# Cross-attention and gated low-rank layer on one core: two turns moved within TensorE's order of a step

## The chip, the cores and the metric

One core of one Trainium2 chip runs the kernel. The metric is the device time of one execution in microseconds (us). The kernel before takes 184.85 us, the median of 3 runs (184.71 to 184.86).

## The reference

1024 tokens (16 batches of 64) of 512 numbers go through two layers, in float32:

```python
x = x + xattn(layernorm(x), ctx, ctx, positions, Wq, Wk, Wv, Wo)
x = x + ffn(layernorm(x), A_w, B_w, Wq_w, keys)
# xattn: 32 heads of 16, 8 heads of k and v; q and k are rotated by position; softmax over 64 keys
# ffn:
q = x @ Wq_w.T; scores = q @ keys.T              # 64 experts
gate = softmax of the 16 largest scores, spread back over the 64
z = x @ A_w.T                                    # 64 experts x rank 8
out = (z * gate) @ B_w.T * 2
```

## The kernel before, in words

The tokens are cut into 8 tiles of 128. A program per engine is written out by hand, and semaphores join them: each `wait_ge` stands in its engine's own order, so a waiting instruction holds up everything behind it on that engine.

Every large product is made in three passes, with both operands split into a rounded high part and a low remainder: high by high, high by low, low by high. `high_part` (L1037 to L1040) issues the first two passes, 8 matmuls of 128x512 for four chunks, and `low_part` (L1042 to L1045) the third, 4 matmuls. ScalarE makes the high part from PSUM, VectorE or GpSimd the low one.

A "turn" is a transpose of 128x128 on TensorE against the identity, with its result in PSUM: `turn_xh` (normalised x, 4 of them, into `ps_t1` in the steps spoken of here), `turn_k` (rotated k, 1, `ps_t0`), `turn_m` (the row maxima of the scores in `m_split`, 2, `ps_t0`), `turn_q`, `turn_x2`, `turn_zg` (gated z, 4, `ps_t1`).

The work is pipelined over the tiles. `first()` and `second()` fill the pipeline, `step(i)` runs for i = 1 to 5, and `last()` empties it. In `step(i)` TensorE works on up to four tiles: the attention of tile i, the scores of n = i+1, the projections of p = i+2, the x turn of i+3, and the gated layer of f = i-2. In step 1 there is no f, so the down product, the turn of z and the up product are left out; in step 5 there is no tile p+1, so the last turn, `turn_xh`, is left out. TensorE's order in `step(i)` before the change is, for i of 2 to 5:

1. `turned_scores(i)` (L1112 to L1126): waits for `mT_ok`, then makes the scores a second time, turned, in tiles of 32 rows, with the negative maxima `mT` added in.
2. `project_down(f, 0)`, `project_q(p, [0, 1])`, `project_down(f, 1)`, `turn_x2(i-1)`.
3. `values(i)`, `turn_q(n)`, `project_kv(p)`, `project_q(p, [2])`.
4. `scores(n, 0)`, `scores(n, 1)`, `turn_zg(f)`.
5. `project_q(p, [3])`, then `turn_k(p)`, then `project_out(i)`.
6. `up_high(f)`, which waits for `q_rot` (VectorE has rotated q of p); `turn_m(n)`, behind a wait for `kT_lo_ok`; `up_low(f)`; `turn_xh(p+1)`.

The next step begins with `turned_scores(i+1)`. What it waits for is made by ScalarE: `m_out(n)` (L486 to L491) copies the turned maxima from PSUM to `mT`. In ScalarE's step stand, in this order: four exponentials with `expert_scores` between the third and the fourth, the z copies, `x2_high`, `q_high`, `values_out`, `o_high`, `k_high(p)` (L472 to L476), `z_high`, `normalise`, `c_high`, `value_blocks`, `m_out(n)`, `x2_centre(i)`, `x_high(p+1)`.

VectorE's step: `x_low`, the statistics of x, `route(f)` (the 16 largest), `x2_low` (L822), `attend(i)` with `q_low(n)` in it, `rotate_k(p)` (L720 to L727), four maxima of the scores (L761), `k_low(p)` (L733), `rotate_q(p)` (L742, L744), `m_parts(n)` (L771, L773), `z_low(f)` (L884), `residual(i)`, `statistics2(i)`, `result(f)`. GpSimd's: `deviation1`, `gated`, `deviation2`, `o_low`, `k_blocks` of the high and of the low part, `rotated_q`, `c_low`. The loads and stores are on SyncE's queue and none of them is in the part of the program that is changed.

Of the kernel before, what the change touches and what calls it, by code (L numbers as in the profile page):

```python
# [51 lines left out]
def build(nc, x, cT, pos, wq, wkv, wo, aT, router, bT, out):  # L52
    ctx = ExitStack()
    with ctx:
# [114 lines left out]
        def kT_bank(t):  # L169
            return (ps_t1 if t < RAW else ps_t0)[:, 0:P]  # L170
# [4 lines left out]
        def up_of(t):  # L175
            return (ps_w0 if t < T - 2 else ps_w1)[:]
# [852 lines left out]
        def _(pe):  # L1029
            def product(dst, hi, lo, w_hi, w_lo, cols, chunks=range(DK)):  # L1030
                for k in chunks:
                    pe.matmul(dst, hi(k), w_hi[:, k, cols], start=(k == 0), stop=False)  # L1032
                    pe.matmul(dst, hi(k), w_lo[:, k, cols], start=False, stop=False)  # L1033
                    mm = pe.matmul(dst, lo(k), w_hi[:, k, cols], start=False, stop=(k == DK - 1))  # L1034
                return mm

            def high_part(dst, hi, w_hi, w_lo, cols, chunks=range(DK)):  # L1037
                for k in chunks:
                    pe.matmul(dst, hi(k), w_hi[:, k, cols], start=(k == 0), stop=False)  # L1039
                    pe.matmul(dst, hi(k), w_lo[:, k, cols], start=False, stop=False)  # L1040

            def low_part(dst, lo, w_hi, cols):  # L1042
                for k in range(DK):
                    mm = pe.matmul(dst, lo(k), w_hi[:, k, cols], start=False, stop=(k == DK - 1))  # L1044
                return mm  # L1045

            def chunk(t):
                return lambda k: t[:, k, :]

            def turn(dst, src, n):  # L1050
                for k in range(n):
                    mm = pe.transpose(dst[:, P * k:P * (k + 1)], src[:, P * k:P * (k + 1)], ident[:])  # L1052
                return mm
# [5 lines left out]
            def turn_xh(t):  # L1059
                pe.wait_ge(xh_ok, t + 1)  # L1060
                turn(xhT_bank(t), xh, DK).then_inc(xhT_ps, 1)

            def project_kv(t):
                if t == RAW:
                    pe.wait_ge(wkv_l, DK)
                pe.wait_ge(c_hi_ok, t - RAW + 1)
                high_part(ps_w1[:, 0:2 * KV], chunk(cT_hi), wkv_hi, wkv_lo, slice(0, 2 * KV))
                pe.wait_ge(c_lo_ok, t - RAW + 1)
                low_part(ps_w1[:, 0:2 * KV], chunk(cT_lo), wkv_hi, slice(0, 2 * KV)).then_inc(kv_ps, 1)

            def turn_k(t):
                pe.wait_ge(k_rot, 3 * t + 3)
                pe.transpose(kT_bank(t), k_r[:], ident[:]).then_inc(kT_ps, 1)

            def project_q(t, chunks):
                if t == RAW:
                    pe.wait_ge(wq_l, DK)
                pe.wait_ge(x_hi_ok, t - RAW + 1)
                pe.wait_ge(x_lo_ok, t - RAW + 1)
                return product(ps_w0[:], chunk(xT_hi), chunk(xT_lo), wq_hi, wq_lo, slice(0, D), chunks)  # L1080

            def turn_q(t):
                pe.wait_ge(q_r_ok, t + 1)
                turn(ps_t0, q_r, REP).then_inc(qT_ps, 1)
# [20 lines left out]
            def turn_m(t):  # L1105
                pe.wait_ge(m_lo_ok, t + 1)
                for rp in range(2):
                    mm = pe.transpose(mT_bank(t)[:, P * rp:P * (rp + 1)],  # L1108
                                      m_split[:, rp].bitcast(F32).rearrange("p c j n -> p (c j n)"), ident[:])
                mm.then_inc(m_ps, 1)  # L1110

            def turned_scores(t):  # L1112
                pe.wait_ge(mT_ok, t + 1)
                for b in range(2):
                    for n, (k, q) in enumerate(((k_bd_hi, qT_hi), (k_bd_lo, qT_hi), (k_bd_hi, qT_lo))):
                        for c in range(PAIRS):
                            rows = slice(QUAD * c, QUAD * (c + 1))
                            pe.matmul(ps_s[:, c, 2 * P * b:2 * P * (b + 1)],  # L1118
                                      k[rows, t % 2, b, 2 * (c % 2):2 * (c % 2) + 2, :].rearrange("p h k -> p (h k)"),
                                      q[rows, t % 2, b].rearrange("p r q -> p (r q)"),  # L1120
                                      start=(n == 0), stop=False)
                    for c in range(PAIRS):
                        rows = slice(QUAD * c, QUAD * (c + 1))
                        mm = pe.matmul(ps_s[:, c, 2 * P * b:2 * P * (b + 1)], sel[rows, b, :],  # L1124
                                       mT[rows].rearrange("p r q -> p (r q)"), start=False, stop=True)
                mm.then_inc(sT_ps, 1)  # L1126

            def values(t):
                pe.wait_ge(exp_ok, 4 * t + 4)
                pe.wait_ge(v_bd_ok, 4 * t + 4)  # L1130
                for b in range(2):
                    for c in range(PAIRS):
                        for h in range(2):
                            rows = slice(ROWS * h, ROWS * (h + 1))
                            mm = pe.matmul(ps_o[QUAD * c:QUAD * (c + 1), h, 2 * P * b:2 * P * (b + 1)],  # L1135
                                           v_bd[rows, t % 2, b, c, :], eT[rows, c, b, :], start=True, stop=True)
                mm.then_inc(o_ps, 1)
# [12 lines left out]
            def project_out(t):  # L1150
                out_high(t)
                out_low(t)

            def turn_x2(t):
                pe.wait_ge(x2_c_ok, t + 1)
                turn(x2T_bank(t), x2_c, DK).then_inc(x2T_ps, 1)
# [12 lines left out]
            def project_down(t, half):  # L1169
                down_high(t, half)  # L1170
                down_low(t, half)

            def turn_zg(t):
                pe.wait_ge(zg_ok, t + 1 if t < T - 1 else T + 1)
                turn(ps_t1, zg, DK).then_inc(zT_ps, 1)

            def up_high(t, chunks=range(DK)):
                if t == 0:
                    pe.wait_ge(b_l, DK)
                pe.wait_ge(zT_hi_ok, t + 1)  # L1180
                high_part(up_of(t), chunk(zT_hi), b_hi, b_lo, slice(0, D), chunks)

            def up_low(t):
                pe.wait_ge(zT_lo_ok, t + 1)
                low_part(up_of(t), chunk(zT_lo), b_hi, slice(0, D)).then_inc(up_ps, 1)
# [72 lines left out]
            def step(i):  # L1258
                f, g, n, p = i - 2, i - 1, i + 1, i + 2
                turned_scores(i)  # L1260
                if f >= 0:
                    pe.wait_ge(x2_ok, i)
                    project_down(f, 0)
                    if f >= 1:
                        pe.wait_ge(res_ok, f)
                    else:
                        pe.wait_ge(q_rot, 2 * p)
                    project_q(p, [0, 1])
                    pe.wait_ge(z_ok, 2 * f + 1)
                    project_down(f, 1)  # L1270
                    turn_x2(g)
                else:
                    pe.wait_ge(q_rot, 2 * p)
                    project_q(p, [0, 1, 2])
                    turn_x2(g)
                values(i)
                turn_q(n)
                if f >= 0:
                    pe.wait_ge(z_ok, 2 * f + 2)
                else:  # L1280
                    pe.wait_ge(x2_ok, i)
                project_kv(p)
                if f >= 0:
                    project_q(p, [2])
                scores(n, 0)
                scores(n, 1)
                pe.wait_ge(x2T_lo_ok, i)
                if f >= 0:
                    turn_zg(f)
                project_q(p, [3]).then_inc(q_ps, 1)  # L1290
                turn_k(p)
                pe.wait_ge(v_st_ok, p + 1)
                project_out(i)
                if f >= 0:
                    pe.wait_ge(q_rot, 2 * p + 2)
                    up_high(f)
                pe.wait_ge(kT_lo_ok, p + 1)
                turn_m(n)
                if f >= 0:
                    up_low(f)  # L1300
                if p + 1 < T:
                    turn_xh(p + 1)

# [64 lines left out]
            for i in range(1, T - 2):  # L1368
                step(i)
# [37 lines left out]
```

## Time and profile before

| what | value |
|---|---|
| median of 3 runs | 184.85 us (184.71 to 184.86) |
| profiled execution, its own time | 184.47 us |
| its span, first to last instruction | 182.5 us |
| granted TensorE clock | 1.00 of full speed throughout |
| TensorE busy (matmuls) | 169.6 us, 93% |
| VectorE busy | 133.0 us, 73% |
| ScalarE busy | 90.0 us, 49% |
| GpSimd busy | 85.6 us, 47% |

A row of the timeline gives the start in us from the span's start, the duration, the engine, the source line, the operation, output and inputs, the shape and how many like it are merged. In square brackets stands how long the engine was idle before the row and what ended that. PE is TensorE's matmuls, PEld its weight loads (a separate track that overlaps the matmuls), ACT ScalarE, DVE VectorE, POOL GpSimd. Matmuls are pipelined: the distance from one start to the next is what a matmul costs, and its duration is longer. A merged row of several matmuls begins with the first and ends with the last one's end. The name `late` is a buffer with four uses (a weight, the second x, z and the gated z).

### The profile page before, as it was taken

To read this page: it belongs to the slowest core of one execution; us is meant where nothing else is said; L and a number is where in the kernel's file an instruction comes from. 1 tells how busy PE (TensorE), PEld (TensorE's weight loads), DVE (VectorE), ACT (ScalarE), POOL (GpSimd) and SP (SyncE) were. 2 spreads that over 40 slices of the span, in tenths; PEclk is the share of its full clock that TensorE was granted. 3 is DMA by queue.
4 is the path that set the end of the run, shared out by engine and by line. 5 is a ranking of instruction groups with operands and counts; after the bars stand their busy time and mean duration, and the time that the engine had idled before them with its cause. 6 is when DMAs were issued, how large, how long until landed. Compare 5 with 4: busy or idle time off the path is not lost.

```text
span 182.5 us, 4057 instructions
## 1 busy us (share of the span) xinstructions
PE 169.6 (93%) x1440; PEld 130.9 (72%) x1440; DVE 133.0 (73%) x391; ACT 90.0 (49%) x206; POOL 85.6 (47%) x109
## 2 busy tenths in 40 slices
PE   7999999988969999999999999999997999599874
PEld 2656575666749887888788878978695767499653
DVE  2667858978994999569954997569938969465461
ACT  3579899636456534742665274644272360432210
POOL 5599989599488349131840275035503020603000
PEclk9999999999999999999999999999999999999999
DMA  5999802001101010101010000100010001000111
GB/s 180 300 400 392 348 4 59 2 12 49 61 3 54 4 57 0 63 0 57 5 57 0 4 0 0 63 0 0 4 57 0 4 0 57 4 4 0 57 57 58
DMA packets 5331, 11.30 MB, mean 62 GB/s; under 512 B 688, under 2 KB 944, under 8 KB 5056
## 3 DMA queue, kind: packets, MB, share of 16 engines
q1 hardware_dynamic: 5024, 10.79, 16.7%
q10 hardware_dynamic: 288, 0.27, 0.4%
q8 instruction: 11, 0.18, 0.4%
q14 instruction: 8, 0.07, 0.1%
HBM read 8.95 MB, written 2.10 MB: 61 GB/s over the span
## 4 chain that ended last, share of the span: by engine, by line
PE 57%; POOL 18%; DVE 10%; issue 10%; DMA 2%; ACT 1%; DVEq 0%; POOLq 0%
PE ps_w L1039 10%; PE ps_w L1044 10%; PE ps_w L1040 9%; PE ps_t L1052 6%; PE ps_s L1099 5%; POOL am_lo L268 3%; PE ps_s L1135 3%; PE ps_s L1118 3%; POOL wo_lo L268 3%; POOL wq_lo L268 2%; PE ps_w L1032 2%; PE ps_w L1033 2%; PE ps_w L1034 2%; POOL k_bd_hi L301 2%; POOL k_bd_lo L301 2%
## 5 line engine op out<-in xcount | busy, mean ns | idle before, releaser
L325 POOL TENSOR_TENSOR late<-late,gate 128x512 f32<-128x512 f32 x7 | 7.6, 1081 | 45.0 <-DVE gate L854 39.3
L310 POOL TENSOR_TENSOR oT_lo<-o_n,oT_hi 128x512 fp32r<-128x512 f32 x8 | 10.3, 1285 | 29.2 <-ACT oT_hi L505 29.2
L761 DVE TENSOR_REDUCE ps_s<-ps_s 128x8 f32<-128x512 f32 x32 | 20.8, 693 | 1.0 <-PE ps_s L1099 0.7
L497 ACT ACTIVATE eT<-ps_s 128x512 f32<-128x512 f32 x32 | 17.0, 598 | 4.1 <-PE ps_s L1124 4.0
L1039 PE MATMUL ps_w<-b_hi,zT_hi 128*128 128x512 f32 (+1 forms) x32 | 12.8, 405 | 1.6 <-ACT zT_hi L545 1.6
L1039 PE MATMUL ps_w<-am_hi,x2T_hi 128*128 128x288 f32 x48 | 13.9, 311 | 0.0
L1040 PE MATMUL ps_w<-am_lo,x2T_hi 128*128 128x288 f32 x48 | 13.1, 296 | 0.0
L505 ACT ACTIVATE oT_hi<-o_n 128x512 fp32r<-128x512 f32 x8 | 5.1, 634 | 14.4 <-DVE o_n L794 14.4
L1040 PE MATMUL ps_w<-b_lo,zT_hi 128*128 128x512 f32 (+1 forms) x32 | 12.1, 381 | 0.0
L1039 PE MATMUL ps_w<-wo_hi,oT_hi 128*128 128x512 f32 x28 | 11.7, 419 | 0.4 <-ACT oT_hi L505 0.4
L1200 PE MATMUL ps_w<-wq_sb,xT_raw 128*128 128x512 f32 x24 | 11.8, 606 | 0.0
L1099 PE MATMUL ps_s<-k_bd_hi,qT_hi 64*128 64x256 f32 x64 | 10.2, 311 | 1.3 <-issue 1.3
L545 ACT ACTIVATE zT_hi<-ps_t 128x512 fp32r<-128x512 f32 x8 | 4.8, 595 | 13.2 <-PE ps_t L1052 13.2
L1040 PE MATMUL ps_w<-wo_lo,oT_hi 128*128 128x512 f32 x28 | 11.1, 395 | 0.0
L779 DVE STREAM_TRANSPOSE o_s<-ps_s 128x1024 f32<-128x1024 f32 x8 | 9.9, 1241 | 0.6 <-PE ps_s L1135 0.6
L1099 PEld LDWEIGHTS ps_s<-k_bd_hi,qT_hi 64*128 64x128 f32 x64 | 6.2, 186 | 5.8 <-issue 5.8
L490 ACT ACTIVATE mT<-ps_t 128x256 fp32r<-128x256 f32 x8 | 3.1, 384 | 14.3 <-PE ps_t L1108 14.3
L1039 PEld LDWEIGHTS ps_w<-am_hi,x2T_hi 128*128 128x128 f32 x48 | 9.0, 187 | 1.2
L291 POOL TENSOR_TENSOR q_r<-q_a,q_b 128x512 f32<-128x512 f32 x7 | 9.0, 1292 | 1.5 <-DVE q_b L744 1.5
L1039 PEld LDWEIGHTS ps_w<-b_hi,zT_hi 128*128 128x128 f32 x32 | 6.0, 188 | 4.8 <-DVE q_b L744 1.8
L301 POOL TENSOR_TENSOR k_bd_lo<-kT_lo,half_mask 128x512 fp32r<-128x512 f32 x8 | 8.8, 1096 | 1.3 <-DVE kT_lo L733 1.3
L1135 PE MATMUL ps_s<-eT,v_bd 64*32 64x256 f32 x256 | 8.8, 382 | 0.6 <-ACT eT L497 0.6
(203 smaller groups left out, 526.4 us busy)
## 6 DMA issues: line engine op xcount, KB each, us to landing
x_sb<-x SPq DMA_DIRECT2D x8, 256.0 KB, 7.2
cT_in<-cT SPq DMA_DIRECT2D x7, 256.0 KB, 2.7
out<-res SPq DMA_DIRECT2D x7, 256.0 KB, 2.0
wq_sb<-wq SPq DMA_DIRECT2D x4, 256.0 KB, 6.4
late<-wo SPq DMA_DIRECT2D x1, 1024.0 KB, 8.3
am_sb<-aT SPq DMA_DIRECT2D x1, 1024.0 KB, 8.5
b_sb<-bT SPq DMA_DIRECT2D x1, 1024.0 KB, 7.1
wkv_sb<-wkv SPq DMA_DIRECT2D x1, 512.0 KB, 4.9
```

Of the source, the lines that this page charges most:

```text
L268: pool.tensor_tensor(lo[:, k, :], raw[:, k, :], hi[:, k, :].bitcast(F32), ALU.subtract).then_inc(low, 1)
L301: pool.tensor_tensor(bd[:, t % 2], kT[:].bitcast(F32).rearrange("p (b q) -> p b q", b=2).unsqueeze(2) .broadcast_to([P, 2, HALF_H, BATCH]) ...
L310: pool.tensor_tensor(oT_lo[:], o_n[:].rearrange("p (b r q) -> p r b q", b=2, r=REP), oT_hi[:].bitcast(F32), ALU.subtract).then_inc(oT_lo_o ...
L497: act.activation(eT[:, c].rearrange("p b n -> p (b n)"), ps_s[:, c, :], ACT.Exp)\
L761: dve.tensor_reduce(neg_top[:, b, HALF_H * half:HALF_H * (half + 1), :], ps_s[:, 2 * (1 - b) + half, :].rearrange("p (r h k) -> p h r k", ...
L1039: pe.matmul(dst, hi(k), w_hi[:, k, cols], start=(k == 0), stop=False)
L1040: pe.matmul(dst, hi(k), w_lo[:, k, cols], start=False, stop=False)
L1044: mm = pe.matmul(dst, lo(k), w_hi[:, k, cols], start=False, stop=(k == DK - 1))
L1052: mm = pe.transpose(dst[:, P * k:P * (k + 1)], src[:, P * k:P * (k + 1)], ident[:])
L1099: mm = pe.matmul(ps_s[:, 2 * (1 - b) + half, 2 * P * rp:2 * P * (rp + 1)], q[rows, t % 2, b, 2 * rp:2 * rp + 2, :].rearrange("p r q -> p ( ...
L1135: mm = pe.matmul(ps_o[QUAD * c:QUAD * (c + 1), h, 2 * P * b:2 * P * (b + 1)], v_bd[rows, t % 2, b, c, :], eT[rows, c, b, :], start=True, s ...
L1200: return pe.matmul(ps_w0[:], xT_raw[:, k, :], wq_sb[:, k, :], start=(k == 0), stop=(k == DK - 1))
```

## The change

`turn_k(p)` goes from behind `project_q(p, [3])` to ahead of it, directly behind `turn_zg(f)`. `up_low(f)` goes from behind `turn_m(n)` to directly behind `up_high(f)`, so that `turn_m(n)` stands directly ahead of `turn_xh(p+1)`. Nothing is added or removed, and no other engine's program changes.

```diff
@@ -1287,17 +1287,16 @@
                 pe.wait_ge(x2T_lo_ok, i)
                 if f >= 0:
                     turn_zg(f)
+                turn_k(p)
                 project_q(p, [3]).then_inc(q_ps, 1)
-                turn_k(p)
                 pe.wait_ge(v_st_ok, p + 1)
                 project_out(i)
                 if f >= 0:
                     pe.wait_ge(q_rot, 2 * p + 2)
                     up_high(f)
+                    up_low(f)
                 pe.wait_ge(kT_lo_ok, p + 1)
                 turn_m(n)
-                if f >= 0:
-                    up_low(f)
                 if p + 1 < T:
                     turn_xh(p + 1)
```

## Rows read from the trace of the kernel before

**Rows 1.** The page: the busy time of TensorE, and the clock it was granted

```profile
PE 169.6 (93%) x1440; PEld 130.9 (72%) x1440; DVE 133.0 (73%) x391; ACT 90.0 (49%) x206; POOL 85.6 (47%) x109
...
PEclk9999999999999999999999999999999999999999
```

**Rows 2.** The list of waits: engine, tile, line, released by: us in total, times, longest

```profile
PEld ps_w L1039 <- DVE q_b L744: 1.8, 4, 0.4
...
ACT late L533 <- PE ps_w L1044: 5.2, 4, 1.6
...
DVE x2T_lo L822 <- ACT x2T_hi L518: 5.8, 5, 1.5
```

**Rows 3.** Timeline of TensorE's matmuls, end of step 4 and start of step 5

```profile
111.21 0.39 PE L1040 MATMUL ps_w<-b_lo,zT_hi 128*128 128x512 f32 x1
111.44 0.38 PE L1108 MATMUL ps_t<-ident,m_split 128*128 128x128 f32 x2
111.58 1.18 PE L1044 MATMUL ps_w<-b_hi,zT_lo 128*128 128x512 f32 x4
112.59 0.60 PE L1052 MATMUL ps_t<-ident,xh 128*128 128x128 f32 x4
113.12 0.39 PE L1118 MATMUL ps_s<-qT_hi,k_bd_hi 32*128 32x256 f32 x4
```

**Rows 4.** Timeline of ScalarE, the same stretch

```profile
111.86 0.38 ACT L490 ACTIVATE mT<-ps_t 128x256 fp32r<-128x256 f32 x1 [2.21 <-PE ps_t L1108]
...
113.23 0.60 ACT L447 ACTIVATE xT_hi<-ps_t 128x512 fp32r<-128x512 f32 x1 [0.23 <-PE ps_t L1052]
114.38 1.57 ACT L497 ACTIVATE eT<-ps_s 128x512 f32<-128x512 f32 x3 [0.56 <-PE ps_s L1124]
```

**Rows 5.** Timeline, end of step 1 (no up product there), TensorE, its loads and ScalarE

```profile
53.22 0.41 PE L1108 MATMUL ps_t<-ident,m_split 128*128 128x128 f32 x2 [1.38 <-DVE m_split L773]
...
53.46 0.60 PE L1052 MATMUL ps_t<-ident,xh 128*128 128x128 f32 x4
...
53.66 0.38 ACT L490 ACTIVATE mT<-ps_t 128x256 fp32r<-128x256 f32 x1 [2.14 <-PE ps_t L1108]
...
54.10 0.19 PEld L1118 LDWEIGHTS ps_s<-qT_hi,k_bd_hi 32*128 32x128 f32 x4 [0.28 <-ACT mT L490]
...
54.70 0.58 ACT L447 ACTIVATE xT_hi<-ps_t 128x512 fp32r<-128x512 f32 x1
```

**Rows 6.** Timeline, end of step 5 and start of the last part

```profile
131.11 0.38 PE L1108 MATMUL ps_t<-ident,m_split 128*128 128x128 f32 x2
...
131.53 0.38 ACT L490 ACTIVATE mT<-ps_t 128x256 fp32r<-128x256 f32 x1 [3.44 <-PE ps_t L1108]
...
132.35 0.19 PEld L1118 LDWEIGHTS ps_s<-qT_hi,k_bd_hi 32*128 32x128 f32 x4 [0.35 <-issue]
...
133.62 1.58 ACT L497 ACTIVATE eT<-ps_s 128x512 f32<-128x512 f32 x3 [0.96 <-PE ps_s L1124]
```

**Rows 7.** Timeline of the last part: ScalarE's copy of the second half of z

```profile
137.44 0.41 ACT L533 ACTIVATE late<-ps_w 128x288 f32<-128x288 f32 x1 [0.27 <-PE ps_w L1044]
```

**Rows 8.** Timeline around the turn of k in step 4: VectorE, the loads, TensorE

```profile
105.20 0.29 DVE L727 TENSOR_TENSOR k_r<-ps_w,k_b 128x128 f32<-128x128 f32 x1
...
105.56 0.19 PEld L1032 LDWEIGHTS ps_w<-wq_hi,xT_hi 128*128 128x128 f32 x1
...
106.38 0.27 PE L1073 MATMUL ps_t<-ident,k_r 128*128 128x128 f32 x1
106.40 0.48 PE L1039 MATMUL ps_w<-wo_hi,oT_hi 128*128 128x512 f32 x1
106.72 0.40 PE L1040 MATMUL ps_w<-wo_lo,oT_hi 128*128 128x512 f32 x1
```

**Rows 9.** Timeline around the turn of k in step 1

```profile
47.84 0.50 PE L1032 MATMUL ps_w<-wq_hi,xT_hi 128*128 128x512 f32 x1
...
48.34 0.29 DVE L727 TENSOR_TENSOR k_r<-ps_w,k_b 128x128 f32<-128x128 f32 x1
```

## The prediction

> **What bounds the kernel now.** I begin with the page: TensorE is busy 93% of the span at full granted clock [rows 1], so the clock has nothing to give and any cost must come from TensorE's order or from a wait in it. The waits say what closes the loop of a step. Four times, once in each of steps 2 to 5, the loads of `up_high(f)` stand idle for up to 0.4 us until VectorE has finished `q_b` (L744). Four times ScalarE waits for `project_down(f, 1)` before it copies the second half of z (L533, up to 1.6 us), and behind that copy, on the same queue, stands `x2_high`, for which VectorE waits up to 1.5 us [rows 2]. So the loop runs: `up_high` starts, TensorE works without a gap through `up_low`, the turns, `turned_scores`, the down products; then ScalarE, then VectorE in one unbroken row from `x2_low` to `rotate_q`; then `up_high` again. Two stretches of TensorE differ in worth. From `up_high` to the end of `project_down(f, 1)` every delay lengthens the step. From there to `up_high` TensorE has a little to spare: its loads normally run about 0.2 us ahead of their product, so of the 0.4 us about 0.2 us is real slack. `turn_k` lies in the second stretch, `turn_m` and `up_low` in the first.
>
> The end of a step is the place to read. In step 4 `turn_m` starts at 111.44, `up_low` at 111.58, `turn_xh` at 112.59, `turned_scores` at 113.12 [rows 3]. ScalarE begins mT at 111.86 and ends it at 112.24 [rows 4], so mT is ready 0.88 us before `turned_scores` starts. That 0.88 us is the cover which `up_low` gives to the copy, and the change takes it away. Steps 2 and 3 repeat the pattern.
>
> **k's turn, steps 2 to 5.** Between products it costs 0.12 us: from 106.38 to the second product at 106.72 is 0.34 us, less one product at 0.23 us (111.21 to 111.44) leaves 0.11 to 0.12 [rows 3, 8]. Two maxima turns cost 1.15 (111.44 to 112.59) less 4 x 0.234 for `up_low` = 0.21 us, 0.11 each [rows 3]. So a turn costs the time of its own weight load wherever it stands, and putting k behind z saves 0.01 us a step. Does it now wait? `k_r` ends at 105.49, and the load that now stands behind the z turn starts at 105.56 [rows 8]: 0.07 us late enough; a miss of 0.1 would fall in the slack of 0.2. What comes earlier is kT_hi on ScalarE, by the 0.70 us of three products, and with it `z_high`, `normalise` and the rest; kT_lo still stands behind VectorE's four maxima, and mT waits for TensorE anyway. `q_ps` comes 0.1 later, long ahead of `rotate_q`. I take 0.
>
> **k's turn, step 1.** There is no z turn to cover it. The loads reach `turn_k` at about 47.84, and `k_r` ends at 48.63 [rows 9]: TensorE stalls about 0.8 us, with `project_q(p, [3])` and `project_out(1)` queued behind. They end 0.8 us later, but TensorE sat idle for 1.38 us ahead of `turn_m`, until VectorE's m_split [rows 5]. Cost 0, with 0.5 us of cover left. If that cover were gone it would be 0.8.
>
> **The maxima, steps 2, 3 and 4.** `up_low` starts where `turn_m` did (its zT_lo was made before) and `turn_m` 0.94 us later than before: 112.38 in step 4. TensorE alone comes out even: 0.94 + 0.21 + the same `turn_xh` brings `turned_scores` to 113.12 again. But mT: ScalarE starts 0.42 after `turn_m` [rows 3, 4], 112.80, takes 0.38, 113.18, and the load of `turned_scores` follows an mT that it waits for by 0.06 (54.04 to 54.10) [rows 5], so 113.24. That is 0.12 later than 113.12. Step 1 is the new order already, since it has no up product: `turn_m` at 53.22, `turn_xh` at 53.46, load of `turned_scores` at 54.10, with 0.28 us idle for mT [rows 5]. Its distance of 0.88 gives 113.26, 0.14 later. I take 0.13 for each, 0.39 for three.
>
> Two rules of the Trainium skill bear on this. The load at 113.12 is natural: it waits until the x turns have run through. "TensorEngine Tiling (Array Packing)", Key Properties, says that a change of tiling mode drains the engine. By that alone the drain would set the start in both orders, and these steps would cost 0 instead of 0.39. "TensorE: Matmul & The Clock Gate", Back-to-back issue gap, gives about 81 ns per matmul of 128 columns in a stream; with it mT would come some 0.03 us sooner in each of four steps, an estimate that puts the sum 0.1 lower. The trace's 0.11 per turn disagrees, and I keep it.
>
> **The maxima, step 5.** There `turn_xh` is left out, so nothing at all stands between `turn_m` and `turned_scores(6)`. Before: `turn_m` at 131.11, mT from 131.53, load of `turned_scores` at 132.35 [rows 6]. After: `turn_m` at 131.11 + 0.94 = 132.05, and 0.86 to 0.88 more gives 132.92. Cost 0.57.
>
> **What is queued behind.** On TensorE, behind the wait for mT, everything, and all of it on the loop. On ScalarE, behind m_out, `x2_centre(i)` and `x_high(p+1)`: with mT begun at 112.80 and the spacing of step 1 (53.66 to 54.70, 1.04) [rows 5], `x_high` begins at 113.84 instead of 113.23 [rows 4] and is done at 114.44; the first exponential, now due at 114.38 + 0.13 = 114.51, just misses it. Cost 0, cover 0.07 us; step 1 again runs so. In the last part ScalarE waits for TensorE at the z copy [rows 7] and had waited 0.96 us ahead of the exponentials [rows 6], so the tail is moved as a whole and absorbs nothing. No DMA moves; the result of f comes 0.2 us earlier and nothing waits for it.
>
> **The sum.** 0 + 0 + 3 x 0.13 + 0.57 = +0.96 us. The profiled execution took 184.47 us (span 182.5), which gives 185.43. The median of the runs stands 0.38 above that execution, so I say 185.8 against 184.85. Bounds of the unknown parts: steps 2 to 4 free, 0.57 in all, 185.4; or each `turn_m` pays on top the 0.10 by which a product behind a turn is spaced wider (0.34 against 0.23 [rows 3, 8]), 4 x 0.10, 186.2. I lean to the lower half of the excess because step 1 shows the whole sequence without it. A measurement of this kernel tells about 0.2% (0.37 us) from no change; "same" means that.
>
> **Rivals.**
> - *Grouping saves the change of kind (faster).* Place: the return from turns to products. Each return costs 0.10 in spacing [rows 8]; if that were a switch and not the turn's load, 4 returns fewer in the first stretch save 0.4 (k's lie under slack): 184.4. It decides only if mT also comes before the x turns end, that is if the 0.86 from `turn_m` to a usable mT shrank below 0.74. For it: the spacing. Against: turns cost 0.11 apiece alone or in pairs, and step 1 waits for mT in just this order [rows 5]. Chance 0.04. "Perfetto Trace Analysis", Matmul Optimizations, asks for matmuls back-to-back in batches so that the engine's power scaling goes well; the clock here is full already [rows 1].
> - *The cover moves, nothing happens.* If the steps were bound by something that TensorE's delay doesn't push, both terms vanish: 184.85. Against: ScalarE and VectorE wait for TensorE in every step [rows 2]. Chance 0.05.
> - *Only step 5 pays.* The mT wait in steps 2 to 4 lies within the draining of the x turns: 185.4. For it: 0.13 us is the difference of two sums of rounded rows. Against: step 1's idle 0.28. Chance 0.10.
> - *k's turn stalls too.* If `k_r` came as late as in step 1 (0.8) in each of four steps, less the slack of 0.2: +2.4, 188.2. It decides once `k_r` ends 0.25 us later against the z turn. Against: `k_r` ends 0.07 us ahead, four times. Chance 0.04, with small amounts the likelier.
>
> **How the numbers follow.** The forecast has the remaining chance, 0.77: 185.8, its own range 185.5 to 186.2. The range takes in "only step 5" (185.4) and 0.1 to each side for the scatter of runs: 185.3 to 186.3. Slower: 0.77 + 0.04 + 0.10, less 0.01 for a small outcome, 0.90. Same 0.06, faster 0.04.
>
> **What would show it.** Right: ScalarE's wait for `turn_m` grows by 0.9 us in steps 2 to 5; the loads of `turned_scores` wait for mT in steps 1 to 5, 0.2 to 0.3 us of idle each and about 0.9 in step 5; the distance from one `turned_scores` to the next grows by 0.13 for steps 2 to 4 and 0.57 for step 5; in step 1 the load of k waits 0.8 us for `k_r` and the wait for m_split shrinks by as much. Wrong: steps of the old length, `turn_m` and `turn_xh` together in under 0.7 us, or a wait of TensorE for `k_r` in the later steps.

## The result, and the profile after

The change makes the kernel slower: 185.44 us median of 5 runs (185.37 to 185.84) against 184.71 us (184.42 to 184.86, 5 runs), a ratio of 1.0047 with a 95% interval of 1.0031 to 1.0062. That is +0.73 us between the medians and +0.90 us between the two profiled executions (184.47 and 185.37 us, spans 182.5 and 183.4).

Ahead of the first `turned_scores`, at about 23 us, stand the loads of the inputs; where this mark falls differs between executions (23.06 to 25.44 us in the thirteen traces of this case). I therefore measure inside the trace, from one `turned_scores` to the next, by the start of its first weight load:

| steps | before, us | after, us | difference | forecast |
|---|---|---|---|---|
| `turned_scores(1)` to `(2)` | 38.13 to 54.10 | 38.07 to 54.05 | +0.01 | 0 |
| step 2 | to 73.78 | to 73.83 | +0.10 | +0.13 |
| step 3 | to 93.43 | to 93.62 | +0.14 | +0.13 |
| step 4 | to 113.12 | to 113.42 | +0.11 | +0.13 |
| step 5 | to 132.35 | to 133.22 | +0.57 | +0.57 |
| first part of the tail | to 145.39 | to 146.27 | +0.01 | 0 |
| sum | 107.26 | 108.20 | +0.94 | +0.96 |

The page after, busy time, and its list of waits (in total, times, longest); they answer to [rows 1] and [rows 2]:

```profile
PE 169.4 (92%) x1440; PEld 130.8 (71%) x1440; DVE 133.4 (73%) x391; ACT 89.7 (49%) x206; POOL 85.4 (47%) x109
...
ACT late L533 <- PE ps_w L1044: 5.2, 4, 1.6
...
PEld ps_s L1118 <- ACT mT L490: 3.0, 7, 0.7
...
PEld ps_w L1039 <- DVE q_b L744: 1.9, 4, 0.5
```

TensorE does the same work, and the waits that close the loop are as before. The third line has grown: the loads of `turned_scores` (L1118) wait for mT seven times instead of three, 3.0 us instead of 1.4.

The end of step 4 after the change, TensorE's matmuls, the first load of `turned_scores`, and ScalarE, beside [rows 3] and [rows 4]. The first row is of the kernel before, the others of the kernel after:

```profile
113.12 0.19 PEld L1118 LDWEIGHTS ps_s<-qT_hi,k_bd_hi 32*128 32x128 f32 x4 [0.17 <-issue]
...
111.63 1.10 PE L1044 MATMUL ps_w<-b_hi,zT_lo 128*128 128x512 f32 x4
112.57 0.38 PE L1108 MATMUL ps_t<-ident,m_split 128*128 128x128 f32 x2
112.78 0.60 PE L1052 MATMUL ps_t<-ident,xh 128*128 128x128 f32 x4
...
113.42 0.19 PEld L1118 LDWEIGHTS ps_s<-qT_hi,k_bd_hi 32*128 32x128 f32 x4 [0.27 <-ACT mT L490]
...
112.98 0.38 ACT L490 ACTIVATE mT<-ps_t 128x256 fp32r<-128x256 f32 x1 [3.86 <-PE ps_t L1108]
...
114.02 0.58 ACT L447 ACTIVATE xT_hi<-ps_t 128x512 fp32r<-128x512 f32 x1
114.69 1.58 ACT L497 ACTIVATE eT<-ps_s 128x512 f32<-128x512 f32 x3
```

`up_low` starts 0.94 us ahead of `turn_m`, and the two maxima turns take 0.21 us (112.57 to 112.78), as they did between products. mT ends at 113.36 and the load follows at 113.42. The natural start, 0.53 us behind the start of `turn_xh` as before, would have been 113.31: the mT wait costs 0.11. The idle times of the load say the same: 0.17 us before, with no wait for mT, and 0.27 now, so only 0.10 of the 0.27 is lost to mT. The exponentials begin at 114.69, 1.27 us behind the load, where the kernel before had 1.26: `x_high` ends at 114.60 and only just stays out of the way.

In step 5 nothing stands between `turn_m` and `turned_scores`, and the whole copy lies bare, beside [rows 6]:

```profile
132.79 0.38 ACT L490 ACTIVATE mT<-ps_t 128x256 fp32r<-128x256 f32 x1 [5.08 <-PE ps_t L1108]
...
133.22 0.19 PEld L1118 LDWEIGHTS ps_s<-qT_hi,k_bd_hi 32*128 32x128 f32 x4 [0.71 <-ACT mT L490]
```

k's turn in step 4, beside [rows 8]: first two rows of the kernel before, then VectorE, TensorE's load and its matmuls after:

```profile
105.18 0.66 PE L1052 MATMUL ps_t<-ident,late 128*128 128x128 f32 x4
105.91 0.40 PE L1033 MATMUL ps_w<-wq_lo,xT_hi 128*128 128x512 f32 x1
...
105.39 0.29 DVE L727 TENSOR_TENSOR k_r<-ps_w,k_b 128x128 f32<-128x128 f32 x1
...
105.74 0.14 PEld L1073 LDWEIGHTS ps_t<-ident,k_r 128*128 128x128 f32 x1
...
105.36 0.66 PE L1052 MATMUL ps_t<-ident,late 128*128 128x128 f32 x4
105.85 0.27 PE L1073 MATMUL ps_t<-ident,k_r 128*128 128x128 f32 x1
105.88 0.48 PE L1032 MATMUL ps_w<-wq_hi,xT_hi 128*128 128x512 f32 x1
106.19 0.39 PE L1033 MATMUL ps_w<-wq_lo,xT_hi 128*128 128x512 f32 x1
```

`k_r` ends at 105.68 and the turn's load starts at 105.74, without a wait. Start of the z turns to the second product is 0.83 us with k among them (105.36 to 106.19) where it was 0.73 without (105.18 to 105.91): the fifth turn costs 0.10 in the group, against 0.12 alone.

Step 1, beside [rows 5] and [rows 9]:

```profile
48.73 0.30 PE L1073 MATMUL ps_t<-ident,k_r 128*128 128x128 f32 x1 [0.88 <-DVE k_r L727]
...
53.17 0.41 PE L1108 MATMUL ps_t<-ident,m_split 128*128 128x128 f32 x2 [0.59 <-DVE m_split L773]
```

TensorE now waits 0.88 us for `k_r`, and its wait for m_split falls from 1.38 to 0.59 us, by 0.79.

### The profile page after: what moved, and what is told of

Its sections match the earlier page's. It is cut to its first block, busy times and chain, and to the rows that moved or that the text cites. A ratio compares the mean times of both kernels' runs of the same rounds, so it can differ in the third digit from the quotient of the medians.

```text
span 183.4 us, 4057 instructions
## 1 busy us (share of the span) xinstructions
PE 169.4 (92%) x1440; PEld 130.8 (71%) x1440; DVE 133.4 (73%) x391; ACT 89.7 (49%) x206; POOL 85.4 (47%) x109
## 4 chain that ended last, share of the span: by engine, by line
PE 57%; POOL 18%; issue 11%; DVE 10%; DMA 2%; ACT 1%; DVEq 0%; POOLq 0%
PE ps_w L1039 10%; PE ps_w L1044 10%; PE ps_w L1040 9%; PE ps_t L1052 6%; PE ps_s L1099 5%; POOL am_lo L268 3%; PE ps_s L1135 3%; PE ps_s L1118 3%; POOL wo_lo L268 2%; POOL wq_lo L268 2%; PE ps_w L1032 2%; PE ps_w L1033 2%; PE ps_w L1034 2%; DMA pos_sb<-pos 2%; POOL k_bd_hi L301 2%
```

## The experiments

All were timed in five rounds beside the kernel before. In these rounds the single times scatter more than in the first comparison (the kernel before alone gave 184.2 to 187.9 us), so an interval is some 0.3 to 0.8% wide and the marks of the traces carry the small differences. Part of the scatter lies outside the kernel's instructions: device time less span (first to last instruction) ranges from 1.7 to 3.7 us. "Marks" is the distance from the load of `turned_scores(1)` to that of `turned_scores(7)`, 107.26 us before and 108.20 after.

**k's turn alone.**

```diff
+                turn_k(p)
                 project_q(p, [3]).then_inc(q_ps, 1)
-                turn_k(p)
```

> Only the turn of k is moved. My theory: 0.0 us (within 0.2). In step 1 TensorE waits 0.9 us for k_r and the wait for m_split shrinks by as much; in steps 2 to 5 the turn costs 0.11 us in either place and lies in the stretch that has 0.2 us of slack. Rival 'k's turn stalls too': slower by 0.2 us or more, with waits for k_r in steps 2 to 5.

Measured: 1.0021, interval 0.9995 to 1.0048. Marks 38.51 to 145.81, 107.30: +0.04 us. In step 1 the picture is that of the whole change:

```profile
49.17 0.30 PE L1073 MATMUL ps_t<-ident,k_r 128*128 128x128 f32 x1 [0.87 <-DVE k_r L727]
53.61 0.41 PE L1108 MATMUL ps_t<-ident,m_split 128*128 128x128 f32 x2 [0.56 <-DVE m_split L773]
```

No other wait for `k_r` is in the list. k's turn costs nothing here; the interval of the times alone would allow up to 0.9 us, the marks of this one trace don't.

**The maxima alone.**

```diff
                     up_high(f)
+                    up_low(f)
                 pe.wait_ge(kT_lo_ok, p + 1)
                 turn_m(n)
-                if f >= 0:
-                    up_low(f)
```

> Only up_low and turn_m are exchanged, k stays where it was. My theory: the whole of the change, +0.9 us: +0.13 in each of steps 2 to 4, +0.57 in step 5. If k's turn had a share of its own, this would lie clearly below or above the 0.9 of the profiled pair.

Measured: 1.0052, interval 1.0033 to 1.0071. Marks 38.74 to 146.89, 108.15: +0.89 us, that is the whole of the change within 0.05.

**The maxima in step 5 alone.**

```diff
                     up_high(f)
+                    if i == T - 3:
+                        up_low(f)
                 pe.wait_ge(kT_lo_ok, p + 1)
                 turn_m(n)
-                if f >= 0:
+                if 0 <= f and i < T - 3:
                     up_low(f)
```

> up_low and turn_m are exchanged in step 5 alone. My theory: +0.57 us, all of it between up_high of step 5 and turned_scores of the last part. Rival, that the small wait of every step makes the loss: near +0.2.

Marks 38.30 to 146.08, 107.78: +0.52 us. Steps 2 to 4 have their old length (19.66, 19.67 and 19.66 us), step 5 has 19.78 instead of 19.23. The ratio of times, 1.0079 with an interval of 1.0052 to 1.0106, is higher than the marks: eight runs from 184.92 to 186.73, of which the profiled one is the lowest and lies 0.45 us above the profiled one of before. The spans settle it: their median is 183.2 us against 182.5 for the kernel before in the same rounds, +0.7, while device time less span is 3.0 us here and 2.0 there. So most of the excess over the marks lies outside the span, and what makes it is not shown; inside, marks and spans agree within the scatter of the start. More than half of the loss is in the one step that has no `turn_xh`.

**The maxima a little less late.** The threshold is the sharpest thing that the theory says, so I tried a place between the two.

```diff
                     up_high(f)
+                    pe.wait_ge(zT_lo_ok, f + 1)
+                    for k in range(3):
+                        pe.matmul(up_of(f), zT_lo[:, k, :], b_hi[:, k, 0:D], start=False, stop=False)
                 pe.wait_ge(kT_lo_ok, p + 1)
                 turn_m(n)
                 if f >= 0:
-                    up_low(f)
+                    pe.matmul(up_of(f), zT_lo[:, 3, :], b_hi[:, 3, 0:D], start=False, stop=True).then_inc(up_ps, 1)
```

> turn_m stands behind three of the four matmuls of up_low instead of behind all four, in steps 2 to 5: 0.70 us later than in the kernel before. My theory is a threshold: the copy to mT has 0.82 us of cover in steps 2 to 4, so those cost 0; in step 5 it has 0.38 us, so that costs 0.70 - 0.38 = 0.32. Sum +0.3 us. A cost in proportion to the distance moved would be 0.75 x 0.9 = +0.7.

Measured: 1.0014, interval 1.0000 to 1.0027. Marks 37.99 to 145.56, 107.57: +0.31 us. Steps 2 to 4 take 19.68, 19.67 and 19.67 us, their old length, though `turn_m` stands 0.70 us later in each. Step 5, TensorE and its first load of `turned_scores`:

```profile
131.67 0.38 PE L1108 MATMUL ps_t<-ident,m_split 128*128 128x128 f32 x2
131.80 0.48 PE L1303 MATMUL ps_w<-b_hi,zT_lo 128*128 128x512 f32 x1
...
132.52 0.19 PEld L1118 LDWEIGHTS ps_s<-qT_hi,k_bd_hi 32*128 32x128 f32 x4 [0.55 <-ACT mT L490]
```

0.85 us from the turn to the load, as in step 4 of the changed kernel (112.57 to 113.42). The cost is a threshold: nothing up to the cover (0.82 us in steps 2 to 4, 0.38 in step 5), then one for one: 0.31 for 0.70 - 0.38 here, and for the 0.94 of the whole change 0.57 in step 5 and 0.10 to 0.14 in the others, where 0.56 and 0.12 are left over.

**VectorE's order in steps 2 to 5.** If TensorE waits for `q_b`, bringing it forward must give the slack back.

```diff
                 top(n, 0)
+                if f >= 0:
+                    rotate_q(p)
                 top(n, 1)
                 k_low(p)
-                rotate_q(p)
+                if f < 0:
+                    rotate_q(p)
                 m_parts(n)
```

> TensorE's order as before; in VectorE's steps 2 to 5 rotate_q goes ahead of the second pair of maxima, so q_b is ready 1.4 us earlier and up_high waits for nothing. My theory of the loop: TensorE's slack of some 0.25 us in each of four steps is gained, -1.0 us. If the loop is bound elsewhere: 0. The wait of up_high's loads for q_b should be gone from the list.

Measured: 0.9926, interval 0.9900 to 0.9953. Marks 38.59 to 144.76, 106.17: -1.09 us; steps 2 to 5 take 19.39, 19.40, 19.40 and 18.96 us, 0.25 to 0.29 less each. VectorE and TensorE in step 4:

```profile
107.26 0.68 DVE L744 TENSOR_TENSOR q_b<-ps_w,cs 128x512 f32<-128x512 f32 x1
...
108.29 1.10 PE L1047 MATMUL ps_w<-wo_hi,oT_lo 128*128 128x512 f32 x4
109.22 0.40 PE L1042 MATMUL ps_w<-b_hi,zT_hi 128*128 128x512 f32 x1
109.46 0.40 PE L1043 MATMUL ps_w<-b_lo,zT_hi 128*128 128x512 f32 x1
```

The up product follows without a gap, and the wait for `q_b` has left the list. So that wait was one that the loop waited for. It also measures the slack: 0.27 us a step, where I had said 0.2.

**VectorE's order in step 1.** There TensorE waits 1.38 us for m_split.

```diff
                 k_low(p)
-                rotate_q(p)
+                if f >= 0:
+                    rotate_q(p)
                 m_parts(n)
+                if f < 0:
+                    rotate_q(p)
```

> TensorE's order as before; in step 1 alone VectorE makes m_parts ahead of rotate_q, so that turn_m's wait of 1.38 us there shrinks by the 1.2 us of rotate_q. My theory: -1.1 us. If what follows in step 2 was late anyhow (x2, the rotated q): less, down to 0.

A miss: 1.0006, interval 0.9970 to 1.0043. `turned_scores(2)` does come early, 14.78 us behind `turned_scores(1)` instead of 15.97 (37.98 to 52.76), but step 2 then takes 21.34 us instead of 19.68 (52.76 to 74.10). The gain of 1.19 is given back with 0.47 on top. VectorE's wait and GpSimd's rows in step 2, the first row from the kernel before:

```profile
58.63 0.18 DVE L702 BATCH_NORM_AGGREGATE mv<-bn 128x2 f32<-128x6 f32 x1 [2.02 <-POOL shift L278]
...
59.01 0.18 DVE L702 BATCH_NORM_AGGREGATE mv<-bn 128x2 f32<-128x6 f32 x1 [2.73 <-POOL shift L278]
...
55.50 2.54 POOL L268 TENSOR_TENSOR b_lo<-b_sb,b_hi 128x512 fp32r<-128x512 f32 x2
57.99 0.56 POOL L275 TENSOR_TENSOR rstd<-ve,neg_half 128x1 f32<-128x1 f32 x1
58.64 0.26 POOL L278 TENSOR_SCALAR shift<-mv,rstd 128x1 f32<-128x1 f32 x1
```

GpSimd still splits B when VectorE wants the statistics; `route` and `x2_low` stand behind that wait on VectorE. The wait was there before too, 2.02 us long. Counted from `turned_scores(1)`, GpSimd's `rotated_q` starts 0.52 us later than before (15.02 against 14.50; 53.00 and 52.63 in the traces), since it waits for the q_b that was put back. That is about as much as the 0.47 that step 2 lost on top.

**Both orders of VectorE (dve_both).**

> Both orders of VectorE together, TensorE as before. My theory: the two gains add, -2.0 us, about 182.7.

Measured: 0.9902, interval 0.9870 to 0.9935, 183.38 us. Marks 38.12 to 144.27, 106.15: -1.11, the gain of steps 2 to 5 and nothing for step 1, for the reason just shown.

**Both, with the change (dve_both_after).**

> Both orders of VectorE with TensorE's order of the change. The maxima's cost of 0.9 us stays. In step 1 the cover of k's stall is gone: turn_m now waits only about 0.2 us before, so of k's 0.8 us stall about 0.6 is paid. My theory: 1.5 us slower than dve_both. If k's stall in step 1 is free under any cover: only 0.9 slower.

Measured: 1.0012, interval 0.9979 to 1.0044, 184.98 us. Marks 40.36 to 147.82, 107.46: 1.31 us above dve_both (1.60 by the medians, 1.5 forecast). `turned_scores(1)` to `(2)` is 0.45 longer (15.22 against 14.77), step 2 0.14, steps 3 and 4 0.09 each, step 5 0.54. So k's stall is paid once its cover is gone, 0.45 us of it and not 0.6. TensorE ahead of `turn_m`, first in dve_both, then here:

```profile
50.71 1.10 PE L1047 MATMUL ps_w<-wo_hi,oT_lo 128*128 128x512 f32 x4
52.01 0.41 PE L1111 MATMUL ps_t<-ident,m_split 128*128 128x128 f32 x2 [0.20 <-DVE m_split L773]
...
53.79 1.09 PE L1047 MATMUL ps_w<-wo_hi,oT_lo 128*128 128x512 f32 x4
54.73 0.38 PE L1111 MATMUL ps_t<-ident,m_split 128*128 128x128 f32 x2
```

Counted from `turned_scores(1)`, these products start 0.84 us later than in dve_both. The cover in dve_both was more than the 0.20 that the row shows: a row lasts longer than its product's spacing, and without a wait `turn_m` starts 0.94 us behind the products (53.79 to 54.73), where in dve_both it starts 1.30 behind. So the cover was 0.36, and 0.84 - 0.36 = 0.48 is the delay of `turn_m` (14.37 against 13.89), of which 0.45 reaches `turned_scores(2)`.

**GpSimd's order alone, with the rest (three_orders), and with the change too.** The last two chunks of B are split in step 2 behind `deviation1`:

```diff
                 if p + 1 < T:
                     deviation1(p + 1)
+                if f == 0:
+                    for k in range(2, DK):
+                        split_lo(b_lo, b_sb, b_hi, b_h, b_l, k)
...
                     c_low(p + 1)
-                if f < 0:
-                    for k in range(2, DK):
-                        split_lo(b_lo, b_sb, b_hi, b_h, b_l, k)
```

> TensorE and VectorE as before; GpSimd makes the low parts of the third and fourth chunk of B (2.5 us) in step 2 behind deviation1 instead of at the end of step 1. My theory: in the kernel before, step 2 waits for these only by way of the normalisation statistics, whose wait ends within 0.3 us of the time at which the step's own loop would be ready: 0 to -0.3 us.

Measured: 1.0005, interval 0.9970 to 1.0040. Marks 38.47 to 145.78, 107.31: +0.05. VectorE's wait of 2.02 us for GpSimd's shift is gone from the trace (L702 starts at 56.99 without one), and nothing is gained: that wait was no limit of step 2 in the kernel before.

> TensorE as before; VectorE's two new orders and GpSimd's. In dve_both the 1.2 us won in step 1 came back in step 2, where VectorE waited 2.7 us for GpSimd, busy with B's low parts until 58.0 us. My theory: with them moved the 1.2 us stay: 1.2 us under dve_both, near 182.2. If something else is late in step 2: no better than dve_both.

Measured: 0.9870, interval 0.9830 to 0.9909, 182.88 us (four runs). Marks 38.55 to 143.96, 105.41: 0.74 us under dve_both, -1.85 against before. VectorE's wait for GpSimd's shift is down to 0.24 us, from 2.72:

```profile
57.10 0.18 DVE L702 BATCH_NORM_AGGREGATE mv<-bn 128x2 f32<-128x6 f32 x1 [0.24 <-POOL shift L278]
...
57.90 0.19 PEld L1042 LDWEIGHTS ps_w<-am_hi,x2T_hi 128*128 128x128 f32 x1 [0.29 <-ACT late L529]
```

The cause was right, the size too large (0.74 us for 1.2): step 2 takes 19.81 us where step 3 takes 19.41. TensorE's loads wait in it for ScalarE's copy of the first half of z (L529), 0.29 us, and another 0.28 ahead of the q product; that part of the 1.2 us goes there is argued from these two, no run removes them. This is the fastest version, and it leaves TensorE's order as it was.

> The same with TensorE's order of the change. My theory: the maxima cost 0.13 + 0.13 + 0.13 + 0.57 = 0.9 us again, and k's turn about 0.45 in step 1 as in dve_both_after: 1.3 to 1.5 us slower than three_orders. If k's turn in step 1 is free: 0.9.

Measured: 0.9941, interval 0.9913 to 0.9969, 183.97 us, 1.1 us above three_orders by the medians. Marks 38.50 to 144.72, 106.22: 0.81 above it. The maxima cost a little less than forecast (steps 3 to 5: 0.08, 0.08, 0.52 for 0.13, 0.13, 0.57). k's stall costs 0.42 us ahead of step 2 (15.20 against 14.78), but step 2 itself is 0.30 shorter (19.51 against 19.81), although the maxima add about 0.1 to it: the wait for L529 is down to 0.17 us and the 0.28 ahead of the q product is gone, so the stall was taken back from the waits for ScalarE. I had expected it to be paid, and the forecast of 1.3 to 1.5 us was at least 0.5 too high by the marks.

## Why the prediction was right, point by point

- *The loop.* Right. The run with q brought forward took 1.09 us off the marks, and the wait of `up_high` vanished. The slack was 0.27 us a step, not 0.2: the 0.17 of late start and the 0.10 by which the unhidden first load spaces the next product. Nothing in the sum hung on it; only the price of the rival *k's turn stalls too* did, which would be 0.3 us smaller.
- *A turn costs its own load wherever it stands.* Right in size: 0.21 us for two maxima turns in the group as between products, 0.10 for k against 0.12. So *grouping saves the change of kind* falls: nothing was saved by standing turns together, and what looked like a wider spacing behind a turn was the price of the turn. That it is the load which sets this price is argued from the equal spacing of the loads (105.74 to 105.85 after), no run separates the two.
- *k's turn, 0 in steps 2 to 5.* Right, and closer than the forecast said. `k_r` ended 0.06 us ahead of the load that needs it, 0.07 in the forecast. But a load that has to wait for `k_r` follows it by 0.05 us (48.63 to 48.68 in step 1 of the kernel before), so only about 0.01 us of that was margin. The loads did keep their spacing (0.38 us from the first z load to the load behind the group, before and after). Had `k_r` come 0.1 us later, the slack of 0.27 would have had to take it.
- *k's turn, 0 in step 1.* Right as a sum and in its parts: a wait of 0.88 us for `k_r` (0.8 forecast), and the wait for m_split 0.79 shorter. The rest of the cover was larger than the 0.5 forecast, about 0.7, since the idle time in a row leaves out some 0.16 us; the pair with both orders of VectorE shows this.
- *The maxima.* Right: +0.10, +0.14 and +0.11 for 3 x 0.13, and +0.57 for 0.57. The run with three of four matmuls ahead of the turn gave +0.31 for the +0.32 that the cover predicts, where a cost in proportion would have been +0.7. That also answers *only step 5 pays*: the step by itself has 0.52 to 0.57 of the 0.94.
- *TensorE's drain.* The start of `turned_scores` is the later of two times: the natural one, 0.53 us behind the start of the x turns, with 0.17 us of idle loads, and mT. The rule of the Trainium skill ("TensorEngine Tiling (Array Packing)", Key Properties) that a change of tiling mode drains the engine gives the first alone; the trace shows 0.27 us of idle loads ended by mT, so the second set it. That the 0.17 us is such a drain no run here shows. The forecast held the whole 0.28 us idle of step 1 against *only step 5 pays*; about 0.17 of it stands there without mT, so its own difference of two sums, 0.12 to 0.14, was the better argument. The 81 ns a turn of the Trainium skill ("TensorE: Matmul & The Clock Gate", Back-to-back issue gap) were not seen: turns in a group cost 0.10 to 0.11 us here.
- *The sum.* +0.96 forecast, +0.94 by the marks, +0.90 between the profiled executions, +0.73 between the medians. The forecast of 185.8 lay 0.36 above the measured 185.44. Of that, 0.06 is the change itself (0.96 against 0.90), and 0.31 the step from a profiled execution to a median: I added the 0.38 of the kernel before, and the five runs after lie 0.07 above their profiled one. That step is scatter and the mechanism says nothing of it; the range of 185.3 to 186.3 had only 0.1 us for it on each side, and 185.44 lies near its lower end.
- *What would show it.* Two details were off. ScalarE's wait for `turn_m` grew by 1.65 us in step 4 (2.21 to 3.86), not 0.9: I left out the 0.7 by which kT_hi and what follows it came sooner, though the text had it. And the loads in step 5 waited 0.71 us, not 0.9.

## What to carry to other kernels

Work that stands between a producer's instruction and the consumer of its copy is cover; before moving it, measure turn-to-usable (here 0.86 us, PE to ScalarE and back) against what is left between, and look for the odd step in which one part of that is absent. Judge a stall by whether its engine waits further on in the same stretch: a wait of 0.88 us was free because one of 1.38 us stood behind it, and gains made by removing such a wait can be taken back at a wait that cost nothing before (VectorE's 2.02 us for GpSimd became the limit of step 2). Grouping small operations saves nothing where the trace shows that each costs its own time wherever it stands.

## What was not expected of the hardware

- The round trip is very regular: 0.85 us from the first maxima turn to the load of `turned_scores` behind a running product, 0.88 us where the turn itself had waited (step 1), in steps far apart and in different executions, so a cost of 0.3 us could be told from one of 0.7 by marks in single traces.
- The start scatters far more than the loop. Between marks kernels with equal steps agree to about 0.05 us; the first mark falls between 23.06 and 23.84 us in twelve of the traces and at 25.44 in one, that of both orders of VectorE with the change. There the granted clock was 0.50 of full speed, the lower level of 1.2 GHz, from 18 to 21 us, falling between 17 and 18 and back at 1.00 from 22 us on, and two products of 128x512 took 1.82 us instead of the 1.12 of dve_both. TensorE had been idle for 1.02 us until 15.10, against 0.39 us in dve_both. Whether that idle time brought the clock down was not tried. All marks from `turned_scores(1)` on were taken at a clock of 1.00.
